# Second attention layer: context evacuated ahead of the exponentials, values weighed ahead of the output projection

## The reference

```
x = x + tanh(g_xattn[0]) * attention0(layernorm(x), ctx)   # 16 heads of 64, a bias on the scores
x = x + tanh(g_ffn[0])   * moe0(layernorm(x))              # 64 experts, 4 per token
x = x + tanh(g_xattn[1]) * attention1(layernorm(x), ctx)   # the layer that changes
x = x + tanh(g_ffn[1])   * moe1(layernorm(x))              # 8 experts, 2 per token, a capacity
```

```
lat = layernorm(latents) * ln_l_w + ln_l_b;   ctx = layernorm(context) * ln_c_w + ln_c_b
q = lat @ Wq;   k, v = split(ctx @ Wkv)       # 256 to 1024, 16 heads of 64
attn = softmax(clip(q k^T / 8, -11, 11));     out = concat_heads(attn v) @ Wo + bo
```

## Time and profile before

| | us |
|---|---|
| median of 3 runs (lowest, highest) | 2045.55 (2044.47, 2047.56) |
| the profiled execution, its own time | 2041.5 |
| its span, first to last instruction | 2039.8 |
| busy: PE, PEld | 1799.8 (88%), 1642.5 (81%) |
| busy: DVE, ACT, POOL | 1244.3 (61%), 901.5 (44%), 601.5 (29%) |

### The profile page before, as it was taken

How to read it: one execution, slowest core, us unless ns; L and a number is a source line. 1 busy time by engine, 2 the same in 40 slices (tenths; PEclk the granted TensorE clock), 3 DMA queues, 4 the chain that set the end, 5 groups by cost and what they waited for, 6 DMA issues and landing times. The chain is left out here.

```text
span 2039.8 us, 47379 instructions
## 1 busy us (share of the span) xinstructions
PE 1799.8 (88%) x16643; PEld 1642.5 (81%) x16643; DVE 1244.3 (61%) x4006; ACT 901.5 (44%) x2276; POOL 601.5 (29%) x731
## 2 busy tenths in 40 slices
PE   6999999999996499967999988989998289999990
PEld 5899999899995488856888877878887289999990
DVE  3567777777777233335777766768776344555545
ACT  4777777777774133323433333423342033333330
POOL 1012232232232200024234333333421254445420
PEclk9999999999998699978999999999998689999996
DMA  6687010011000589972232111111100142222106
GB/s 229 248 273 258 27 42 37 26 39 38 26 30 24 167 284 299 295 240 79 84 110 69 48 43 50 38 46 51 51 25 23 58 158 94 88 79 83 52 33 252
DMA packets 134144, 214.13 MB, mean 105 GB/s; under 512 B 16878, under 2 KB 85009, under 8 KB 133952
## 3 DMA queue, kind: packets, MB, share of 16 engines
q1 hardware_dynamic: 106560, 147.89, 21.6%
q0 software_dynamic: 23040, 59.58, 8.9%
q10 hardware_dynamic: 4352, 4.20, 0.6%
HBM read 111.88 MB, written 103.68 MB: 106 GB/s over the span
## 5 line engine op out<-in xcount | busy, mean ns | idle before, releaser
L467 POOL DMA_INDIRECT buf<-a_rxn,a_disp x192 | 197.0, 1026 | 241.2 <-DVE comb L882 102.8
L621 ACT ACTIVATE a_S<-a_S,a_mn 128x128 f32<-128x128 f32 x512 | 198.9, 395 | 45.5 <-DVE a_mn L912 45.5
L82 PE MATMUL e_psH<-e_x_hi,e_w_hi 128*128 128x256 f32 x640 | 181.9, 284 | 0.0
L83 PE MATMUL e_psH<-e_x_lo,e_w_hi 128*128 128x256 f32 x640 | 178.7, 279 | 0.0
L84 PE MATMUL e_psH<-e_x_hi,e_w_lo 128*128 128x256 f32 x640 | 178.5, 279 | 0.0
L603 ACT ACTIVATE a_kT<-a_psP 128x512 f32<-128x512 f32 x128 | 75.7, 593 | 208.3 <-PE a_psP L84 208.3
L82 PE MATMUL a_psP<-a_c_hi,a_wk_hi 128*128 128x256 f32 x512 | 157.4, 307 | 9.8 <-DVE a_c_lo L774 9.7
L82 PE MATMUL a_psP<-a_x_hi,a_wq_hi 128*128 128x256 f32 x512 | 155.9, 305 | 5.2 <-DVE a_x_lo L774 5.2
L1207 PE MATMUL a_psM<-a_wo,a_oT 128*128 128x256 f32 x512 | 123.7, 397 | 30.6 <-ACT a_plain L564 23.4
L83 PE MATMUL a_psP<-a_c_lo,a_wk_hi 128*128 128x256 f32 x512 | 148.2, 290 | 0.0
L84 PE MATMUL a_psP<-a_c_hi,a_wk_lo 128*128 128x256 f32 x512 | 148.2, 290 | 0.0
(11 more groups left out here) (203 smaller groups left out, 5464.1 us busy)
## 6 DMA issues: line engine op xcount, KB each, us to landing
buf<-a_zeros SPq DMA_DIRECT2D x16, 1320.0 KB, 8.6
buf<-a_zeros SPq DMA_DIRECT2D x16, 1024.0 KB, 6.0
e_rows<-buf SPq DMA_DIRECT2D x64, 256.0 KB, 3.9
e_w_in<-in_L_ffn_w SPq DMA_DIRECT2D x64, 256.0 KB, 3.2
y<-e_y SPq DMA_DIRECT2D x64, 256.0 KB, 3.2
a_ctx<-in_ctx SPq DMA_DIRECT2D x32, 256.0 KB
e_w_out<-in_L_ffn_w SPq DMA_DIRECT2D x64, 128.0 KB, 3.8
y<-a_zeros SPq DMA_DIRECT2D x32, 256.0 KB
```

What stands on the lines that cost most here:

```text
L82: pe.matmul(dst, a_hi, b_hi, start=start, stop=False)
L83: pe.matmul(dst, a_hi, b_lo, start=False, stop=False)
L467: g_.indirect_dma_start(out=buf, out_offset=bass.IndirectOffsetOnAxis(ap=disp[:, par, i, k:k + 1], axis=0), in_=rxn[:, par, i], in_offset= ...
L621: ins = a.activation(s[:, h], s[:, h], ACT.Exp, bias=mn[:, u % 2, h:h + 1], scale=-1.0, accum_out=z[:, u % 2, h:h + 1])
```

## The change

On ScalarE, in step 3 of the second layer, `evac_ctx` moves ahead of the exponentials of the step's first unit. On TensorE, in all steps of the second layer, the two calls of `weigh_turned` move ahead of `project_out`; this matters in steps 1 and 3, where `project_out` does something. No instruction is added or removed, and no wait is changed. The first layer keeps its orders.

```diff
@@ -646,8 +646,10 @@
                     evac_heads(g, w)
                 if proj:
                     evac_job(plus(g, 1), 1 - par, EARLY[w][0])
+                if not first and prep and w == 3:
+                    evac_ctx(plus(g, 2))
                 exponentials(g, 2 * w)
-                if prep and w == 3:
+                if first and prep and w == 3:
                     evac_ctx(plus(g, 2))
                 if proj:
                     evac_job(plus(g, 1), 1 - par, EARLY[w][1])
@@ -1229,10 +1231,14 @@
                     router_inputs(plus(g, -1), 1 - par)
                 if proj and w == 0:
                     transpose_x(plus(g, 1))
-                project_out(g, w, proj, prep)
-                weigh = weigh_values if first else weigh_turned
-                weigh(g, 2 * w, par)
-                weigh(g, 2 * w + 1, par)
+                if first:
+                    project_out(g, w, proj, prep)
+                    weigh_values(g, 2 * w, par)
+                    weigh_values(g, 2 * w + 1, par)
+                else:
+                    weigh_turned(g, 2 * w, par)
+                    weigh_turned(g, 2 * w + 1, par)
+                    project_out(g, w, proj, prep)
 
             def router_inputs(g, par):
                 pe.wait_ge(s_rxn, at(g, 1, 1))
```

## The result

The changed kernel takes 2020.69 us (median; 2020.58 to 2021.65), the kernel before 2046.55 us on the same chip: a ratio of 0.9876 (95% interval 0.9857 to 0.9895). The forecast, 2035.0 us, had the sign right and the gain too small by more than half; the range ended at 2024 us. The profiled execution of the changed kernel took 2021.65 us, 19.9 us less than that of before.

The account below looks back on a forecast made before the run. The second layer was taken as bound by TensorE, gapless but for 12 waits for ScalarE in step 3. Gains of 14.1 us less 1.1 and 2.5 gave 10.5 us: 2045.55 to 2035.0 us, range 2024 to 2046.

Parts of the forecast that it names:

- nine groups (of 2 to 13) without a loop end behind them: Second layer: five groups inside the loop gain 1.11 us each, four outside it 1.2 us each.
- three groups with one: Second layer, groups at the three loop ends: 1.22 us gained each, 3.7 us in all.
- steps before the first wait, and behind group 14: Groups 1 and 14, where nothing was stalled: new waits in step 2 cost 0.5 + 0.64 = 1.1 us.
- end of the layer: Groups 14 and 15: the later update costs 1.45 us in step 2 of group 15 and 0.54 us twice, 2.5 us.
- the third wait: TensorE's new wait for VectorE before the transposes of x in step 0: 0.11 us a group inside the loop.
- the 12 waits: TensorE's waits for ScalarE before step 3's output projection, groups 2 to 13: all go, 26.4 us to be had.
- waits for VectorE at lines 1068 and 1178: New TensorE waits: 0.64 us at the router's transposes, 0.40 at step 3's weighing, 0.11 at the transposes of x.
- VectorE waiting longer for the projection: In step 1 the projection comes behind the weighing, so VectorE's update of x waits 1.45 us longer.
- VectorE did not have room: Rival: VectorE has slack for the later update of x; gain 17 to 24 us, 2024.5 us, chance 0.14.
- The ring: Rival: the mutual waits of TensorE and VectorE eat the gain; gain 0 to 4 us, 2044.4 us, chance 0.16.
- ScalarE's move cost nothing: Step 3: the moved evacuation runs in ScalarE's 3.08 us of idle without delaying the exponentials, with 1.4 us of cover.
- the clock fell: Rival: short waits make TensorE's clock fall once a group, 1.69 us each, 23.7 us lost; 2058.7 us, chance 0.10.

Follow-up runs that it names:

- step-3 form: Both edits, but weighing goes ahead of the projection in step 3 only, against the kernel before: 2009.18 us (0.9827); with 128 waits added to move its code, 2005.54 us.
- ScalarE's edit alone: The kernel before with only the context's evacuation moved ahead of the exponentials, TensorE's order kept: 2017.4 us, ratio 0.9859.
- turn-end form: The kernel before, weighing ahead of the projection only in the last step of each loop turn: 2025.09 us (0.9901); code moved by 128 waits: 2020.22 us (0.9872).
- three loop kernels whose turns end in the weighing: The kernel before, 2046.55 us; the same with 128 waits added to move its code, 2043.5 us; ScalarE's edit alone, 2017.4 us.
- the four kernels written out: Second layer's loop written out, no loop ends: kernel before 2029.76 us, changed kernel 2007.53, step-3 form 1995.74, ScalarE's edit alone 1991.54.

## Why the prediction was wrong, and where it was right

Second layer, profile against profile, in us gained:

| term | forecast | measured |
|---|---|---|
| nine groups (of 2 to 13) without a loop end behind them | 5.6 + 4.8 = 10.4 | 7.8 |
| three groups with one | 3.7 | 14.4 |
| steps before the first wait, and behind group 14 | -1.1 | -2.4 |
| end of the layer | -2.5 | -2.3 |
| the start, and half clock in one step each of groups 0 and 15 | none | 3.3 |
| sum | 10.5 | 20.8 |

The phase behind the layer took 0.8 us longer, so the whole execution gained 19.9 us.

**The step that failed** is "Behind the three loop ends TensorE stands about 4.5 us, so there the third wait falls away: 1.22 us gained." I took the row without a releaser for a fixed price that the change couldn't reach, and never asked what ends it. It is TensorE's sequencer at the back edge of a loop (the branch from a turn's end to its start), waiting for code. The change puts the 16 long matmuls at the end of the turn, so the sequencer branches with 3.60 us of work still before the array instead of 0.72, and the wait lies under that work. The forecast of 3.7 us for these three groups became 14.4. Shown by the step-3 form against ScalarE's edit alone (fetches at every end in both, 4.5 against 14.0 us) and by the turn-end form with and without its code moved. Of the 14.4 us, 1.7 are the half clock of group 5, which did not come after. In the changed kernel itself run-ahead had a fetch to hide only at the second end; at the first and third there was none, and how much the order and how much the missing fetch gave there no run separates.

The Trainium skill ("Runtime: NRT & Kernel Launch", "Instruction fetch mechanics") would have named the row: it says that a taken branch whose target lies outside the current window of two pages of code has to fetch the target's page before execution goes on. The traces agree where they fetch (3.8 to 4.8 us of idle in the three loop kernels whose turns end in the weighing). They differ on what stays: two pages are 512 instructions by that section, which also gives TensorE room for 2048, but the turn-end form ran turns of 1800 instructions, and the first layer's loop turns of 1498, without a fetch of TensorE's code at their ends.

**What is late next at a loop end** is VectorE. Its timeline there in the kernel before, and then in the changed one:

```profile
1266.03 0.74 DVE L746 TENSOR_SCALAR a_xn<-a_xn,a_mv,a_rstd 128x256 f32<-128x256 f32 x2 [2.86 <-issue]
```

```profile
1257.04 0.79 DVE L748 TENSOR_SCALAR a_xn<-a_xn,a_mv,a_rstd 128x256 f32<-128x256 f32 x2 [2.74 <-issue]
```

At its three ends it stands 2.6 to 2.9 us in both. I read that as its own branch, since its work resumes 3.1 to 3.3 us after its sequencer branches at the second end, but no run tests it. Before, that lay inside TensorE's longer stall; now the transposes of x wait for it (1.17 us above, 2.3 and 2.2 at the others). Hence 21.62 us in both turn-end forms: their gaps at the scores, 0 and 0.12 us, are made up by waits of 1.32 and 1.12 us at the transposes.

**The steady state** went as forecast in mechanism: the 12 waits gone, waits for VectorE at lines 1068 and 1178 (now 1070 and 1180), VectorE waiting longer for the projection. The gain was 0.88 instead of 1.11 us a group inside the loop, because two terms were missing. The turned order costs TensorE 0.19 us in each step where it projects, with no wait at all: step 3 of group 1 takes 11.12 us against 10.93 in the earlier trace rows. Two such steps a group are 0.38 us. And each new wait at line 1070 cost about 0.2 us more than its idle: steps 0 and 2 of group 9, with waits of 0.18 and 0.27 us, took 0.37 and 0.48 us longer than before. The prediction had charged such a start, 0.25 us, to the old wait alone. With 0.16 us at the weighing of group 8 the waits of this turn came to 0.61 us, not 1.15: 2.26 - 0.38 - 0.61 - 0.40 = 0.87 us.

**The rivals.** VectorE did not have room, though the time (2020.69) lies beyond that rival's 2024.5. The ring did not close. ScalarE's move cost nothing, as forecast. Between the layer's first and last group the clock fell in one step of the changed kernel only (behind a wait of 2.2 us at the third loop end, 0.93 above). The Trainium skill's rule ("TensorE: Matmul & The Clock Gate", "A second HAM failure mode: psum-queue depth-cycling") that I weighed there was not borne out for the short waits: some twenty of 0.2 to 0.4 us and no fall. It was the old 2 us waits that carried this price, and the profile of before, with one fall in twelve, was a lucky one: its time lies 4 to 5 us below the medians of its runs, which spread over 13 us (2041.5 to 2054.6), while the changed kernel's spread over 1.1. That falls make this spread fits (1.69 us each), but was not tried by itself.

**Open:** why a loop of 1800 instructions is fetched anew in every turn in one form, in every other in another, and never in a third. Moving the code makes a difference (none to every turn in the turn-end form), but the loops of the kernel before and of the turn-end form start at the same place, a turn of the second is one wait shorter, and they differ. Nor did any run have this layer's turn end in short work with its code resident; only the first layer's loop shows that case.

## What to carry to other kernels

A wait with no releaser at a loop's back edge is a cost to explain before anything near it is moved: ask how far the engine's sequencer is ahead of its work when it branches, and how long the branch itself lasts in the trace; let a turn end in the engine's longest instructions, or write the loop out if it has few turns. Where one engine is late (here ScalarE), repair that alone first: beside it the second edit cost 0.9 us a group and had its worth only where it hid the branch. Price a wait with the clock that follows it, over several profiles: a step with the same wait of some 2 us was 2.3 us longer in one profile and 3.8 in another.

## What the runs showed of the hardware

- The back edge of the loop of 1800 instructions lasts 3.3 to 5.1 us on TensorE's sequencer when code is fetched at it, 0.2 us when none is. With the fetch TensorE idles 3.8 to 4.8 us, some 6 us with the lower clock behind it, when its last work is short (0.72 us); 0.1 to 2.0 us when the sequencer is 3.4 to 3.6 us ahead. VectorE stands 2.6 to 2.9 us at the same ends in the kernel before and the changed one.
- Reading straight-line code costs nothing that shows: the four kernels written out fetch 103 blocks of TensorE's code (109 in the kernel before) and are 13 to 26 us faster than with the loop.
- How often a wait of some 2 us was followed by the lower clock differed from profile to profile: one of 12, three and four of eight, six and 10 of 12, at 1.5 to 1.7 us each. There is one profile of each kernel, so what decides it is open.
- A wait of 0.1 to 0.4 us on TensorE cost about 0.2 us more than its idle.
- Turning long matmuls behind short ones costs TensorE 0.19 us a step with no wait in it.
